# A graph-network kernel: VectorE's order within a group, and one bias addition taken from GpSimd to VectorE

## The reference

```python
h = relu(layernorm(x))
m = concat([h[src], h[dst], edge_attr]) @ mW1 + mb1        # 320 -> 256, one row for each edge
m = relu(relu(m) @ mW2 + mb2) @ mW3 + mb3                  # 256 -> 256 -> 128
summed = segment_sum(m, src) + segment_sum(m, dst)         # back to the 1024 nodes
x = x + mlp3(concat([h, summed, attention(h)]), uW1, ub1, uW2, ub2, uW3, ub3)
h = relu(layernorm(x))
x = x + gelu(gcn(h @ W, src, dst) + b)                     # normalised by the node degrees
```

## Time and profile before

| | |
|---|---|
| median of three runs | 767.0 us (766.85 to 767.35) |
| profiled execution, its own time | 765.72 us |
| its span in the trace | 763.9 us |
| granted TensorE clock, mean | 0.994 |
| busy: TensorE, VectorE | 736.0 us (96%), 729.5 us (96%) |
| busy: GpSimd, ScalarE | 539.0 us (71%), 524.3 us (69%) |

### The profile page before, as it was taken

One profiled execution on the slowest core, in us unless ns is written; L12 is line 12 of the kernel. 1 busy time (PEld: TensorE's weight loads), 2 busy tenths in 40 slices (PEclk: granted clock), 3 DMA queues, 4 the chain that ended last, 5 costly groups with the idle time before them and its releaser, 6 DMA issues.

```text
span 763.9 us, 13342 instructions
## 1 busy us (share of the span) xinstructions
PE 736.0 (96%) x4171; PEld 619.3 (81%) x4171; DVE 729.5 (96%) x1506; ACT 524.3 (69%) x711; POOL 539.0 (71%) x533
## 2 busy tenths in 40 slices
PE   7589999999999999999999999999999999999896
PEld 6467888888888888888888888888888888888755
DVE  7889999999999999999999999999999999999775
ACT  3256777777777777777777777777777777776623
POOL 3777777777777777777777777777777777777100
PEclk9899999999999999999999999999999999999999
DMA  7534444344434444344443444434443444432000
GB/s 227 164 119 129 128 127 123 117 126 129 126 112 125 130 128 127 114 124 128 127 124 113 130 129 126 126 112 127 129 126 113 126 127 130 126 111 83 0 1 28
DMA packets 42566, 90.15 MB, mean 118 GB/s; under 512 B 11136, under 2 KB 17920, under 8 KB 42496
## 3 DMA queue, kind: packets, MB, share of 16 engines
q0 software_dynamic: 24576, 67.14, 28.6%
q1 hardware_dynamic: 17920, 22.16, 9.9%
HBM read 86.64 MB, written 2.62 MB: 117 GB/s over the span
## 4 chain that ended last, share of the span: by engine, by line
PE 88%; DVE 4%; POOL 3%; issue 2%; DMA 2%; ACT 1%; DVEq 0%; SPq 0%; POOLq 0%
PE bank L628 30%; PE bank L607 22%; PE bank L617 14%; PE bank L587 7%; PE bank L593 7%; PE bank L646 4%; POOL rows_sb L446 2%; POOL rows_sb L454 1%; DVE ring L1005 1%; PE bank L720 1%; DMA w_sb<-mW 1%; PE bank L765 1%; PE bank L728 1%; DMA table_a<-rows_sb 0%; PE bank L714 0%
## 5 line engine op out<-in xcount | busy, mean ns | idle before, releaser
L446 POOL DMA_INDIRECT rows_sb<-table_a,ends_i x256 | 263.5, 1029 | 82.2 <-issue 77.7
L454 POOL DMA_INDIRECT rows_sb<-table_b,ends_i x256 | 262.7, 1026 | 78.0 <-issue 78.0
L812 ACT ACTIVATE dist<-iota_h,neg_mid 128x1026 f16<-128x1026 f16 (+1 forms) x256 | 292.3, 1143 | 0.0
L1005 DVE TENSOR_SCALAR ring<-dist,half_gap,times 128x1026 fp32r<-128x1026 f16 (+1 forms) x256 | 276.4, 1081 | 1.7 <-ACT dist L812 0.6
L628 PE MATMUL bank<-ring,m_hi 128*128 128x512 f32 x512 | 172.4, 418 | 1.3 <-DVE ring L1005 1.1
L802 ACT ACTIVATE h_sb<-bank,b_sb 128x512 f32<-128x512 f32 x128 | 87.6, 684 | 122.5 <-PE bank L607 122.5
L628 PE MATMUL bank<-ring,m_lo 128*128 128x512 f32 x512 | 160.8, 395 | 0.0
L607 PE MATMUL bank<-ring,w_hi 128*128 128x512 f32 x512 | 150.0, 394 | 1.4 <-DVE ring L985 1.4
L1057 DVE TENSOR_SCALAR oh_key<-iota_h,key_f,minus_base 128x258 bf16<-128x258 f16 x321 | 128.5, 400 | 0.0
L617 PE MATMUL bank<-w_sb,h_sb 128*128 128x128 f32 x1024 | 124.8, 275 | 0.0
L593 PE MATMUL bank<-ident,rows_sb 128*128 128x128 f32 x512 | 113.7, 276 | 8.0 <-DVE rows_sb L1048 8.0
(11 more groups left out here) (182 smaller groups left out, 628.5 us busy)
## 6 DMA issues: line engine op xcount, KB each, us to landing
e_raw<-edge_attr_t SPq DMA_DIRECT2D x128, 128.0 KB, 3.1
rows_sb<-table_a,ends_i POOLq DMA_INDIRECT x256, 2.8
rows_sb<-table_b,ends_i POOLq DMA_INDIRECT x256, 2.9
table_a<-rows_sb SPq DMA_DIRECT2D x4, 256.0 KB, 3.4
table_b<-rows_sb SPq DMA_DIRECT2D x4, 256.0 KB, 2.5
x_sb<-x SPq DMA_DIRECT2D x2, 256.0 KB, 3.2
out<-oh_key SPq DMA_DIRECT2D x4, 128.0 KB, 1.8
u_sb<-uW SPq DMA_DIRECT2D x1, 384.0 KB, 5.0
```

Source lines behind the costliest of these rows:

```text
L446: nc.gpsimd.indirect_dma_start(got[:, b, t, 0, :], None, table_a, bass.IndirectOffsetOnAxis(ap=ends_i[:, 0, tile:tile + 1], axis=0),).then ...
L454: nc.gpsimd.indirect_dma_start(got[:, b, t, 1, :], None, table_b, bass.IndirectOffsetOnAxis(ap=ends_i[:, 1, tile:tile + 1], axis=0),).then ...
L812: nc.scalar.activation(to, of, ACT.Abs, bias=neg_mid[:, bass.ds(g * GT + t, 1)]).then_inc(dist_ready, 1)
L1005: nc.vector.tensor_scalar(to, of, half_gap[:, tile], times[:, tile], ALU.is_equal, ALU.mult).then_inc(inc_ready, 1)
```

## The change

VectorE's order in a step becomes

```diff
-    IN_ROWS = (0, 2)
+    IN_ROWS = (0, 1)
...
-            pool.wait_ge(ld_w, 16 * 12)
-            nc.gpsimd.tensor_tensor(xb_sb[:, :, :], x_sb[:, :, :],
-                                    ub3_all[:, :].unsqueeze(1).broadcast_to([P, NC, D]), ALU.add).then_inc(xb_ready, 1)
...
                 if makes:
                     tile0 = window_tile(i + 1)
-                    one_hots(i + 1, tile0, b, (0, 1))
+                    one_hots(i + 1, tile0, b, (0,))
+                if nxt:
+                    add_pair(g + 1, 0)
                 if past:
                     incidence(g - 1, 1)
                 if nxt:
-                    add_pairs(g + 1)
+                    add_pair(g + 1, 1)
                 if makes:
-                    one_hots(i + 1, tile0, b, (2,))
+                    one_hots(i + 1, tile0, b, (1, 2))
                 if past:
                     incidence(g - 1, 2)
+                if nxt:
+                    low_first(g + 1, 1 - b, 0)
                 if exists(g + 2):
                     low_edges(g + 2, b)
                 if nxt:
-                    low_first(g + 1, 1 - b, 0)
+                    low_first(g + 1, 1 - b, 1)
                 if past:
                     incidence(g - 1, 3)
                 if makes:
-                    one_hots(i + 1, tile0, b, (3,))
-                if nxt:
-                    low_first(g + 1, 1 - b, 1)
-                if makes:
-                    one_hots(i + 1, tile0, b, (4,))
+                    one_hots(i + 1, tile0, b, (3, 4))
                 if now:
                     incidence(g, 0)
                     low_messages(g, b)
                 if summed_in(b, i):
                     window_sums(i)
+                if g == 0:
+                    biased_rows()
+
+            def biased_rows():
+
+                dve.wait_ge(ld_w, 16 * 12)
+                nc.vector.tensor_tensor(xb_sb[:, :, :], x_sb[:, :, :],
+                                        ub3_all[:, :].unsqueeze(1).broadcast_to([P, NC, D]), ALU.add).then_inc(xb_ready, 1)
```

More of the change, by code:

```diff
@@ L1038, in group, with add_pair @@
                     window_sums(i)
-            def add_pairs(g):
-                b, n = g % GB, g // GB
[L1043 to L1049, removed]
+                if g == 0:
[4 more added lines that the diff above has]
+                                        ub3_all[:, :].unsqueeze(1).broadcast_to([P, NC, D]), ALU.add).then_inc(xb_ready, 1)
+            def add_pair(g, half):
+                b, n = g % GB, g // GB
+                tiles = slice(2 * half, 2 * half + 2)
+                for t in (2 * half, 2 * half + 1):
+                    dve.wait_ge(ga_done[b][t], 16 * (n + 1))
+                    dve.wait_ge(gb_done[b][t], 16 * (n + 1))
+                nc.vector.tensor_tensor(got[:, b, tiles, 0, :], got[:, b, tiles, 0, :], got[:, b, tiles, 1, :],
+                                        ALU.add).then_inc(pair_added, 1)
             def window_tile(w):
```

## The result

The changed kernel takes 776.37 us (median of 4 runs, 775.46 to 777.55) against 766.92 for the kernel before beside it: a ratio of 1.0127, interval 1.0108 to 1.0145. It is slower by 9.45 us; the forecast was 6.8. The profiled execution took 775.46 us with a span of 773.7, which is 9.8 over the span before.

What follows compares the result with a forecast made beforehand. TensorE was taken to set the pace, 21.33 us per two steps, with VectorE close behind. Steady steps +5.7, start +0.9 and end +0.2 gave +6.8 on 767.0, so 773.8 us, range 767.7 to 782.

Steps and rivals of the forecast that it cites:

- The pace of before: Mid-run, kernel before: TensorE sets the pace, 10.66 us a step, so no VectorE order can make a step shorter.
- The loop: VectorE's second add through TensorE and ScalarE back to `low_first` 1: play shrinks to 0.17, costing 0.19 us per step pair.
- the detour: From VectorE's second add over TensorE's transposes and ScalarE's `relu_first` 1 to `low_first` 1: 3.55 us.
- The steady term: Loss in mid-run, odd steps 3 to 61: 30 times 0.19 us, +5.7 us.
- The steady steps: Mid-run passage: VectorE's work per step stays the same, only its meeting points with other engines shift; +5.7 us.
- GpSimd becomes the bound: Mid-run rival: spread adds and flat incidences hold gathers, rows land late; round 21.8, 782 us in all; chance 0.16.
- The play suffices: Mid-run rival: steps stay at 10.66 us, only start and end count, 768.1 us; chance 0.18.
- GpSimd is the hidden pace: Mid-run rival: gathers set today's pace, the new order frees them, 5 us faster, at most 762; chance 0.08.
- The start: Steps 0 and 1: bias on VectorE makes the second add, which TensorE awaits, later: +0.9 us, between +0.4 and +1.2.
- The end: Last steps: no GpSimd bias addition holding VectorE, but a slower incidence form for tile 1; net +0.2 us.
- the -0.2 for GpSimd's addition: Near the end: GpSimd's addition no longer holds up VectorE's flat incidence, -0.2 us, between 0 and -2.2.
- +0.4: Step 64: TensorE waits for incidence 1, later in its three-row form; +0.4 us, between 0 and +0.9.

Runs made afterwards that it cites:

- e5: Kernel before, without the second table's gathers of tiles 0 and 2 from group 3 on: 767.16 us, ratio 1.0008.
- e8: Kernel before with only the bias addition moved to VectorE at the end of step 0: 767.18 us, ratio 1.0009.
- e9: Kernel before with the last bias added by VectorE just ahead of the residual near the end: 766.45 us, ratio 0.9995.
- e11: Changed kernel with `low_first` 1 behind incidence 3 and without the second table's gathers of tiles 0 and 2 from group 3 on: 768.63 us, ratio 1.0024.
- e4: Changed kernel without the second table's gathers of tiles 0 and 2 from group 3 on: 774.57 us, ratio 1.0099.
- e3: Changed kernel with `low_edges` moved behind `low_first` 1: 806.08 us, ratio 1.0511.
- e13: Kernel before with only the new incidence forms (tiles 0 and 1 three-row, tile 2 flat), old order and bias: 777.11 us, ratio 1.0135.
- e7: Changed kernel with the bias addition back on GpSimd behind the gathers: 773.85 us, ratio 1.0096.
- e2: Changed kernel with `low_first` 1 moved behind incidence 3: 774.16 us, ratio 1.0096.
- e1: Changed kernel with the old incidence forms back (tile 1 flat, tile 2 three-row), new order and bias kept: 771.37 us, ratio 1.0053.
- e12: Changed kernel with the old incidence forms and without the second table's gathers of tiles 0 and 2 from group 3 on: 768.10 us, ratio 1.0022.
- e6: Changed kernel with the second of the two window sums made in the odd steps: 779.07 us, ratio 1.0162.

## Why the prediction was right, and where it wasn't

**The pace of before.** Right. TensorE's 10.66 a step is a floor (e5, e8, e9 and e11 all have 21.34 a round); no run here, whatever VectorE's order, has a shorter one.

**The loop.** Right, term by term: 7.35 for 7.31 on VectorE, 10.86 for 10.86 with the detour, 21.530 for 21.52 where it acts alone (e4), and 22.553 for 22.54 where it was tightened (e3). Alone it makes +5.57 from step 3 to step 61 (705.84 - 81.46 = 624.38 against 618.81), where the forecast had 5.7 in 30 rounds.

**What it left out.** The steady term was +7.40. The step that failed is the first sentence of "The steady steps": a three-row and a flat incidence change places, the rest only moves. VectorE's work is the same, but gathers are held where they meet it, and e13 shows that the exchange of forms alone costs 8.95 (627.76 - 618.81), with rows that land late. In the changed kernel both bounds act in one round: 5.57 from the loop, and 0.4 (e7) to 1.8 more, since rows land late in even steps, where the loop has no play. The two don't add: the gathers alone cost 5.08 (e2).

**The rival "GpSimd becomes the bound"** was treated as an alternative, with 0.16, that excludes the forecast. It holds beside it. Its threshold, 21.66 at a third of each add and flat incidence, is near the measured 21.59, but that tests nothing: gathers that stand back to back fill whatever the round is, 21.34 before and 22.55 in e3, where after the start no add waits for them. The price of 782 was too high. Had the loop been left open, this rival would have been the result (e2: 774.16, of which 5.08 in the rounds). That the forecast came near thus owes something to luck, two bounds of nearly the same size. All three of its terms came out larger: 7.40 for 5.7, 1.87 for 0.9, 0.53 for 0.2.

**The play suffices, GpSimd is the hidden pace.** Both are out, the first by e3 and e4, the second by e5.

**The start.** The adds came where they should, 0.67 late for 0.9, but by two misses that cancel in part, both of which the prediction had named as bounds: the gathers landed 0.55 earlier (42.91 for 43.46), and from there to the second add of step 1 VectorE took 11.02 (53.93 - 42.91) where the sum had 10.72, with a wait of 0.20 for ScalarE. Step 3 came 1.87 late. The other 1.20 go with the lower clock, for which the sum had no term: from the second add of step 1 to step 3 it takes 26.36 here (80.29 - 53.93), and 25.04 in e7 (79.13 - 54.09) and 25.02 in e11 (80.66 - 55.64), where the granted clock from 54 to 58 us is 1.00. The idle times of 1.90 and 1.19 at these adds don't explain the fall: e11 has 1.89 and 1.19 at the same adds and no fall, and by e9 it can also come without the change. So the term can't be settled finer than from 0.7 (e7) to 1.9.

**The end.** With the old forms the -0.2 for GpSimd's addition came out: with the bias off GpSimd the rest behind step 61 is 66.44 to 66.49 (e1, e8, e9, e12), against 66.67, all good to 0.1, since spans are given to a tenth. (e1 and e12 have the new order too.) With the new forms it doesn't show: the rest is 67.20 in the changed kernel and 67.16 in e7, which has GpSimd's addition still. The new forms were sized a little low: they cost 0.5 (67.16 - 66.67) to 0.7 (67.20 - 66.47) for +0.4. Step 63's four incidences take 4.93 in all, beside the diagonal addition, where before they took 4.55. With the old order and the new forms (e13) the rest is 67.90, and no run shows why. From 726 to 730 us the changed kernel's granted clock is 0.61, and 1.00 in the kernel before; e8 and e9 have such a stretch too (0.59 from 718 to 722, 0.57 from 720 to 724), and their rest is no longer for it.

What stays open: why the new forms with the old order (e13) hold gathers longer than with the new order (e2). And e13 wasn't run with fewer gathers, nor was e6, so that their causes rest on their waits for rows and aren't shown by a run.

## What to carry to other kernels

Where two engines meet in a loop of results, add up the way of each between the meeting points, and for unequal steps go around once: the difference of the sums is the play, and when it is gone the price can be worked out, here to a few hundredths. Then ask for each other queue that is never idle whether it has room, and test it by taking work away from it: GpSimd's gathers stood back to back before and after, and taking a quarter of them away gave nothing in the kernel before, 1.8 in the changed kernel (e4) and 5.5 in the one with its loop opened (e2 to e11). And try parts of a change alone: the smallest edit of this one, two numbers in a tuple, costs as much as the whole.

## What the runs showed of the hardware

Gathers and VectorE hold each other. An undisturbed gather takes 0.94; behind adds, one-hots and a flat incidence it took 2.21 (e13), and a flat incidence that met a gather took 0.84 instead of 0.72 (e1). By the Trainium skill's page "SBUF — State Buffer", section "Who interferes with whom", the order of issue decides which of the two engines blocks, not the shape of the operation. These rows show the delay on either side, but not that order, as far as starts in the rows tell: the gather of e13 began at 302.51, ahead of the adds at 302.62, and was held, and the flat incidence of the earlier trace rows began at 701.88, ahead of GpSimd's addition at 701.91, and was held. So where the prediction says that the trace agrees, it does so for the length of the delay, 2.2, alone.

In mid-run, with the row of flat incidence and two adds broken up, the longest gather is shorter, but not the sum: two gathers lost 0.40 each on average where one had lost 0.65.

TensorE's granted clock fell to 0.57 in the window behind two idle times of 1.90 and 1.19 us, with stretches at the lower of its two levels, and a pair of matmuls took 1.20 for 0.72. It fell to 0.60 in e9, behind 1.48 and 1.02. But it stayed at 1.00 in e7 with 0.75 and 1.19, and in e11 with 1.89 and 1.19:

```profile
54.00:58.00 4.00, 2.27 (x14) 1.75 (x15) 4.00 (x9) 1.14 (x2) 3.09 (x4) 1.00 0.30 80
```

So the idle times at these adds don't tell by themselves whether the clock falls.
